# A transformer layer with routed experts on one core: the loads of the split expert matrices move from SP's DMA queue to ScalarE's

## What is computed

```python
# attention (16 heads, 4 key/value heads, causal, softmax kept chunk by chunk)
q = (x @ wq); k = (x @ wk); v = (x @ wv)
out = chunked_attention(q, k, v)          # exp(scores - max), sum, times v
x = layernorm(x + out @ wo)
# experts (8 experts, top 2 per token)
logits = clip(x @ gate_w.T, -50, 50)
top_w, top_idx = top_k(logits, 2);  rw = softmax(top_w)
deltas = softmax(expert_atom_weights) @ atoms
weighted = deltas * sigmoid(importance)   # 8 x 4096 entries
vals = einsum('tk,tks->ts', rw, weighted[top_idx])
contrib = segment_sum((x[:, cols] * vals).T, rows)   # rows, cols = mask_idx // 512, % 512
x = layernorm(x + x @ W.T + contrib.T)
```

## Time and profile before

| | |
|---|---|
| median of three runs | 1959.86 us (1957.28 to 1963.02) |
| the profiled execution's own time | 1953.45 us |
| its span (first to last instruction) | 1951.7 us |
| PE busy | 1844.5 us (95%) |
| DVE, POOL, ACT busy | 1232.1 (63%), 839.7 (43%), 810.6 us (42%) |
| share of the chain that ended last: PE, DVE, DMA | 76%, 6%, 4% |
| expert weights: loads, size, median time to landing | 8 of 2048 KB, 12.1 us |

### The profile page before, as it was taken

How to read it: one execution, slowest core, us unless ns; L and a number is a source line. 1 busy time by engine, 2 the same in 40 slices (tenths; PEclk the granted TensorE clock), 3 DMA queues, 4 the chain that set the end, 5 groups by cost and what they waited for, 6 DMA issues and landing times.

```text
span 1951.7 us, 33846 instructions
## 1 busy us (share of the span) xinstructions
PE 1844.5 (95%) x9525; PEld 1562.0 (80%) x9525; DVE 1232.1 (63%) x3804; ACT 810.6 (42%) x2001; POOL 839.7 (43%) x1172
## 2 busy tenths in 40 slices
PE   7899999999999999999999889999899998999991
PEld 7788888888888888888888777877788887877871
DVE  3445547775777577757776677677676774663444
ACT  1244434443444344434444444444444442333443
POOL 6265434433433343343333333233323333777764
PEclk9999999999999999999999999999999999999996
DMA  8543363334333333343335554545544348546777
GB/s 294 168 167 135 119 228 118 118 111 144 113 119 116 139 115 124 109 137 124 109 109 173 163 162 162 198 139 173 173 156 155 124 162 323 174 156 212 245 274 291
DMA packets 151972, 318.75 MB, mean 163 GB/s; under 512 B 18904, under 2 KB 62184, under 8 KB 140840
## 3 DMA queue, kind: packets, MB, share of 16 engines
q1 hardware_dynamic: 132320, 273.06, 40.4%
q0 software_dynamic: 19472, 43.49, 7.1%
HBM read 226.38 MB, written 90.12 MB: 162 GB/s over the span
## 4 chain that ended last, share of the span: by engine, by line
PE 76%; DVE 6%; issue 4%; DMA 4%; POOL 3%; ACT 1%; SPq 1%; POOLq 0%; DVEq 0%; ACTq 0%
PE psum L1256 21%; PE psum L1257 20%; PE psum L1258 20%; PE psum L1283 7%; PE psum L1926 3%; PE psum L1928 2%; PE psum L1927 2%; DMA route_rows<-attn_residual 2%; DVE piece_lo L1626 1%; PE psum L249 1%; POOL chosen_rows L1872 1%; DMA expert_weights_hi_lo<-split_expert_weights 1%; DMA token_rows<-x,ids_now 1%; ACT probs L1507 1%; SPq L1025 1%
## 5 line engine op out<-in xcount | busy, mean ns | idle before, releaser
L1158 POOL TENSOR_SCALAR probs<-probs,row_inv 128x128 f32<-128x128 f32 (+3 forms) x512 | 306.4, 630 | 449.4 <-DVE row_inv L1623 446.6
L1507 ACT ACTIVATE probs<-probs,neg_max 128x512 f32<-128x512 f32 (+3 forms) x512 | 282.6, 556 | 359.3 <-DVE neg_max L1615 357.2
L1256 PE MATMUL psum<-xT_hi,w_hi 128*128 128x512 f32 x640 | 253.3, 396 | 6.8 <-PEq L643 3.7
L1258 PE MATMUL psum<-xT_hi,w_lo 128*128 128x512 f32 x640 | 251.3, 393 | 0.0
L1257 PE MATMUL psum<-xT_lo,w_hi 128*128 128x512 f32 x640 | 250.8, 392 | 0.0
L1615 DVE CUSTOM_DVE_ANT_0 probs<-psum,causal 128x512 f32<-128x512 f32 (+3 forms) x512 | 222.8, 486 | 33.2 <-PE psum L1258 14.0
L1256 PE MATMUL psum<-wo_hi,oT_hi 128*128 128x512 f32 x512 | 209.2, 409 | 31.3 <-DVE y_acc L1654 29.4
L1626 DVE TENSOR_TENSOR pT_lo<-psum,pT_hi 128x512 fp32r<-128x512 f32 (+1 forms) x384 | 206.2, 592 | 22.2 <-ACT pT_hi L1517 22.0
L1517 ACT CAST pT_hi<-psum 128x512 fp32r<-128x512 f32 (+1 forms) x384 | 172.2, 526 | 96.3 <-PE psum L1283 96.3
L1258 PE MATMUL psum<-wo_hi,oT_lo 128*128 128x512 f32 x512 | 204.4, 399 | 0.0
L1257 PE MATMUL psum<-wo_lo,oT_hi 128*128 128x512 f32 x512 | 204.3, 399 | 0.0
(11 more groups left out here) (201 smaller groups left out, 4052.5 us busy)
## 6 DMA issues: line engine op xcount, KB each, us to landing
w_hi<-split_qk_weights SPq DMA_DIRECT2D x140, 256.0 KB, 2.7
w_lo<-split_qk_weights SPq DMA_DIRECT2D x140, 256.0 KB, 3.0
wo_hi<-split_out_weights SPq DMA_DIRECT2D x28, 1024.0 KB, 4.9
wo_lo<-split_out_weights SPq DMA_DIRECT2D x28, 1024.0 KB, 7.0
expert_weights_hi_lo<-split_expert_weights SPq DMA_DIRECT2D x8, 2048.0 KB, 12.1
x_in<-in_L_attn_x_dram SPq DMA_DIRECT2D x8, 1024.0 KB, 6.8
expert_weights<-fill_sb SPq DMA_DIRECT2D x4, 2048.0 KB, 7.7
attn_residual<-y_acc SPq DMA_DIRECT2D x8, 1024.0 KB, 4.5
```

Source lines behind the costliest of these rows:

```text
L1158: last = pool.tensor_scalar(p, p, row_inv[:, buf, i:i + 1], 1.0, ALU.mult, ALU.mult)
L1256: pe.matmul(dst, hi_s, hi_m, start=start, stop=False)
L1258: return pe.matmul(dst, lo_s, hi_m, start=False, stop=stop)
L1507: last = act.activation(probs[:, buf, a:a + w], probs[:, buf, a:a + w], ACT.Exp, bias=neg_max[:, buf, i:i + 1], scale=-1.0, accum_out=row_ ...
```

## The change

`load_expert` moves from SP's program to ACT's, so that the eight loads go into ACT's own DMA queue. Their places:

- expert 0: before, on SP at the end of the iteration (batch 7, g = 0); now on ACT in iteration g = 1, behind the exponentials `exps(n + 1, 1)`
- experts 1 and 2: before, on SP near the start of the last iteration; now on ACT behind `exps(n + 1, 1)` of that iteration, with the same waits
- 3 and 4: behind `pT(n + 1, 1)`. 5: behind `exps(n + 3, 1)`. 6 and 7: behind the last `oT_half`. SP had waits of its own ahead of these (`s_q`, `s_qk`, `s_o`). ACT has by then waited for the same events in its list.

Nothing else is changed: SP keeps its other loads and stores in their order.

```diff
@@ SP (sync)
-        def load_expert(e):
-            sp.dma_start(E.d[:, e]..., d_kept[e]...).then_inc(E.s_d_in[e], 16)
...
             slot(3, it + 1, after)
-            if kind == "end":
-                sp.wait_ge(s_seed, NB)
-                sp.wait_ge(s_xt, NB * C)
-                sp.wait_ge(s_vg, 2 * NIT)
-                load_expert(1)
-                sp.wait_ge(E.s_tables, 1)
-                load_expert(2)
-                sp.wait_ge(s_q, NIT * G)
-                load_expert(3)
-                load_expert(4)
             if route:
                 route_store(sp, R, it - TT, R.x1_dram[bass.ds((it - TT) * P, P), :])
...
-            if job == "last":
-                if g == 0:
-                    for kept in s_piece_out:
-                        sp.wait_ge(kept, 32 + 16 * PIECES)
-                    sp.wait_ge(s_v, NB * TT)
-                    load_expert(0)
-                if g == HKV - 1:
-                    sp.wait_ge(s_qk, 3 * NIT * G)
-                    load_expert(5)
-                    sp.wait_ge(s_o, NIT * G)
-                    load_expert(6)
-                    load_expert(7)
@@ ACT (scalar)
+        def load_expert(e):
+            act.dma_start(E.d[:, e]..., d_kept[e]...).then_inc(E.s_d_in[e], 16)
...
             exps(n + 1, 1)
+            if job == "last" and g == 1:
+                for kept in s_piece_out:
+                    act.wait_ge(kept, 32 + 16 * PIECES)
+                load_expert(0)
+            if kind == "end":
+                act.wait_ge(s_seed, NB)
+                act.wait_ge(s_xt, NB * C)
+                act.wait_ge(s_vg, 2 * NIT)
+                load_expert(1)
+                act.wait_ge(E.s_tables, 1)
+                load_expert(2)
...
             pT(n + 1, 1)
+            if kind == "end":
+                load_expert(3)
+                load_expert(4)
...
             exps(n + 3, 1)
+            if kind == "end":
+                load_expert(5)
...
             if kind != "end":
                 exps(n + 4, 0)
             else:
+                load_expert(6)
+                load_expert(7)
                 high_tokens(act, E, psum, 0)
```

More of the change, by code:

```diff
@@ L1033, in keep_piece @@
                              ).then_inc(s_piece_out[step % 2], 16)
-        def load_expert(e):
-            sp.dma_start(E.d[:, e].rearrange("p s c n -> p s (c n)").bitcast(F32),
-                         d_kept[e].rearrange("s p n -> p s n")).then_inc(E.s_d_in[e], 16)
         def slot(j, use, g):
@@ L1540, in high_piece @@
             act.copy(F.piece_hi[:, k], F.piece_raw[:, k].rearrange("p (r e) -> p e r", e=NE)).then_inc(s_piece_hi, 1)
+        def load_expert(e):
+            act.dma_start(E.d[:, e].rearrange("p s c n -> p s (c n)").bitcast(F32),
+                          d_kept[e].rearrange("s p n -> p s n")).then_inc(E.s_d_in[e], 16)
         def v(b, t):
```

## The result

The changed kernel takes 1965.70 us (median of 8 runs, 1962.26 to 1969.78), the kernel before, timed beside it, 1960.11 (8 runs, 1957.28 to 1963.02). The ratio is 1.0029, 95% interval 1.0017 to 1.0040. A repeat gave 1.0018 (1.0008 to 1.0029): 1964.23 against 1960.55. So the change costs 3.7 to 5.6 us, 0.2 to 0.3%: both intervals lie above 1. The profiled execution took 1964.12 us, with a span of 1962.3.

A forecast was written before the change was run, and what follows sets the result against it. PE was taken to bound the kernel, through the passage between its two stages. First tile +3.1 us, less 2.45 us of low clock, gave +0.7 us: 1954.2 profiled, 1960.6 on the median, range 1957 to 1964.

The forecast's parts named there:

- What bounds it, and where the stall goes: Passage between the stages: PE bounds; the 4.88 us stall before the first expert tile moves ahead of `out_rows`, not removed.
- ACT's own time: ACT's seven issues in the passage: 0.45 us each assumed, costing 0 to 0.1 us because DVE's rows hide them.
- The stream's start and the gap: Expert loads: start 5.1 us later, DMA gap of 1620 to 1624 filled for 2.0 us back; last landing 1648.0.
- The wo fetch: `wo` on SP's queue beside ACT's experts: about half the rate, landing +5.0 us, PE restarting at 1634.7.
- Rows 8: Profile rows of POOL's gathers beside SP's experts, 209 to 235 packets: queues share near one to one by packets.
- The meeting point: First expert tile: starts at the later of 1649.1 (`out_rows`) and 1649.8 (experts), +3.1, less 2.45 for its clock: +0.7 us.
- the low clock: PE's clock falls after a long idle time; the products that follow take 2.45 us longer, first expert tile or `out_rows`.
- the third rival: `wo` at a third of the rate or less; decides from a PE restart after 1635.4; 1965 or more; chance 0.18.
- The base: Profiled execution of the kernel before, 1953.45 us, first tile at low clock; forecast carried to the median 1959.86.
- The second stage: PE's expert tiles behind 1652: moving the first tile moves the end by as much, within POOL's and DVE's slack.
- a `wo` served behind all experts: Extreme of the rival on `wo`: fetched only after all ACT's expert loads, some +14 us, 1974.

The follow-up runs named there:

- act_early12: The changed kernel with experts 1 and 2 issued on ACT ahead of the last iteration's exponentials; 1962.40 us, ratio 1.0024 to the kernel before.
- act_567: The kernel before with only expert loads 5, 6 and 7 moved to ACT, at the changed kernel's places; 1959.14 us, ratio 1.0006.
- five_first: The kernel before, all loads on SP, with expert 5 issued ahead of the `wo` fetch; 1961.59 us, ratio 1.0006.
- sp_567: The changed kernel with expert loads 5, 6 and 7 put back on SP behind the `wo` fetch; 1961.32 us, ratio 1.0001 to the kernel before.
- after_rows: The changed kernel with `wo` fetched in two parts and heads 0 and 1 of two row tiles done first; 1967.53 us, ratio 1.0032 to before.
- wo_rows: The kernel before with `wo` fetched in two parts and heads 0 and 1 of two row tiles done first; 1961.60 us, ratio 1.0003.

## Why the prediction was right, and where it was not

The forecast was +0.7 us on 1959.86, no change that a measurement can tell; measured were +3.7 and +5.6, still within 0.3%. That it stayed there was in part luck: 1965.70 is outside the prediction's own range of 1957 to 1964 and at the very border, 1965.7, where it begins to say slower. The share of the queues, the place of the stall and ACT's time were right; the size was not. Step by step:

- **What bounds it, and where the stall goes: right.** One stall ahead of `out_rows`, none ahead of the first tile, the clock at 0.50 behind the restart, and a first tile of 2.8 us (1649.99 to the next turn at 1652.81 in the chain).
- **ACT's own time: right, for another reason.** The issues took 0.37 to 0.53 us. They cost nothing not because DVE's rows hide them, but because the sequencer makes them while earlier ACTIVATEs run.
- **The stream's start and the gap: nearly right, 1.3 us too late.** +5.1 - 2.0 = +3.1 was forecast for the last landing, and +1.8 was measured (1646.7 against 1644.90). The issue came at 1599.05 + 1.13 = 1600.2, 1.2 us ahead of the forecast 1601.34, and that is nearly all of it.
- **The wo fetch: the share right, the landing mis-sized.** Rows 8 gave one to one, and 112 to 112 was measured. But 14.3 - 6.9 = +7.4 us, not +5.0. Left out was the time until the first packet, 3.3 us behind a full queue against 1 before; the difference, 2.3, is the missing 2.4. PE restarts at 1635.87 + 1.13 = 1637.0, not 1634.7.
- **The meeting point: this step failed.** The forecast let `out_rows` be ready at 1649.1, just ahead of the experts at 1649.8. With `wo` 2.3 us later and the experts 1.3 us earlier (1646.7 + 1.77 = 1648.5 is when they would let PE start), `wo` alone decides, and nothing waits behind it to swallow the low clock. The prediction's rule for the third rival (from a restart after 1635.4 on each us counts) gives 1637.0 + 2.45 + 11.47 + 0.5 = 1651.4; the tile started at 1649.75 + 1.13 = 1650.9. So that rival's rule held, though its condition, a third of the rate or less, did not: `wo` had half.
- **The base.** The sum stood on one profile of before, in which the first tile paid 2.45 us of low clock. In the repeat it did not, and there is no such saving: the passage is 2.1 us longer than in the first profile and 4.4 than in the second, where the forecast had 0.7. How often each case comes among the timed runs was not measured; the timed differences, 3.7 and 5.6, fit the second better.
- **The second stage** shows no cost beyond its own spread. From the first to the 42nd expert result took 150.79 us in after, 148.65 in its repeat, 149.24 in the repeat of before and 146.2 to 150.8 in the experiments. The first profile of before has 139.85 there and stands alone. So the two first spans, 1962.3 and 1951.7, overstate the change, and I draw nothing from their difference.
- **Slips without effect.** By the prediction's own steps a `wo` served behind all experts gives 1647.7 + 11.47 + 2.45 + 0.5 + 2.76 = 1664.9, +13 and 1973, not +14 and 1974. And PE has a fourth idle time in the passage, 0.40 us at 1615.59 behind DVE, the same in every kernel.

Passage minus PE's idle time in it is 41.1 to 42.2 us in every run of the table but `act_early12` (42.8, where the clock was low behind the stall ahead of the anchor as well), so the passage follows the sum of PE's waits. The Trainium skill, "DMA: Bandwidth & Descriptors", section "Issuing engines are not separate DMA queues", says that a second issuing engine saves issue time only; `act_567` and `five_first` agree (passages 46.52 and 46.60). The section "Queues, rings and completion order" of the same page has each DMA engine change queues by the packet; 112 to 112 at equal packets, and 148 to 157 at 3.6 against 7.4 KB, agree. Neither section says anything of a first packet held up behind another queue's backlog, and here the measurement decides. What makes that delay stays open: it was seen in every profile where SP issued a load behind a busy queue of ACT and had none of its own under way (`wo` in after, its repeat, `sp_567`, `act_early12` and `after_rows`; `route_rows` in `act_early12`), and no run separated its cause.

## What to carry over

A transfer that an engine will soon wait for should not be asked for while another queue is full: in these runs neither queue had priority, the late one started about 3 us later and then shared by packets, so the one with the smaller packets got less. Within one queue the order is a choice, and a stall can be made smaller there by splitting the fetch and by doing first the products that need only its first part. Where two waits follow each other, work out both ends before moving bytes: in `wo_rows` PE saved under a microsecond on the first wait and paid more on the second (6.41 against 4.88 us), and in the changed kernel the second wait went and the first grew by more.

## What the runs showed of the hardware that was not expected

- A queue's first packets behind another queue's backlog moved about 3 us after the issue (1621.06 to about 1624.4; 1593.10 to about 1596.6; in `sp_567` 1623.66 to about 1626.6), against 1 us at 1622.25 before. In `sp_567` ACT's queue had some 1.4 MB left at the issue and in the changed kernel some 3.5 (loads issued less what the queue had moved), and the pause was nearly as long; so it is not the time until that queue is empty.
- ACT's DMA issues run ahead of its ACTIVATEs: issued at 1599.05, inside the ACTIVATE of 1598.66, though the list has them behind the last ACTIVATE that begins at 1599.64.
- In two profiles of one kernel an idle time of 1.75 us left the granted clock at 1.00, and one of 1.85 us was followed by 0.50, 1.2 us after the restart. The prediction leaned on the first; it has no margin.
- Where the low clock falls decides whether it costs: in the two profiles of before, ahead of a wait nothing that shows, behind it some 2.4 us (passages 46.12 and 48.48).
